# A top-k search over experts moved from 80 lists on partitions to 125 nodes on partitions, with its ranks and its list products rearranged

## What is computed

```python
x = x + gnn(layernorm(x), src, dst, edge_attr, ...)   # 41250 edges, messages summed per node
h = layernorm(x)
S = softmax(h @ Wg, axis=-1)                          # 1250 nodes x 8 experts
G, I = top_k(S.T, 312)                                # for each expert its 312 highest nodes
ex = h[I]                                             # 8 x 312 x 512
out = gelu(ex @ W1[e] + b1[e]) @ W2[e] + b2[e]        # 512 -> 1024 -> 512
x = x.at[I].add(G[..., None] * out)
```

## Time and profile before

| what | value |
|---|---|
| median of 3 runs | 1441.53 us (1441.02 to 1441.79) |
| the profiled execution | 1442.35 us |
| its span in the trace | 1440.5 us |
| TensorE matmul busy | 1323.8 us, 92% |
| VectorE busy | 1027.4 us, 71% |
| mean granted TensorE clock | 0.951 |
| search, first to last instruction | 1078.10 to 1108.64 us |
| ranks, to the end of `pos` | to 1116.03 us |
| first product of the first expert | 1132.35 us |

### The profile page before, as it was taken

The page is one execution under the profiler, slowest core; times in us unless marked ns, Lnnn a source line. Parts: engine busy times, 40 slices in busy tenths (PEclk is TensorE's granted clock), DMA queues, the critical chain, the costliest instruction groups (busy, mean ns, idle before and its releaser), DMA issues. The chain is left out here.

```text
span 1440.5 us, 26692 instructions
## 1 busy us (share of the span) xinstructions
PE 1323.8 (92%) x7075; PEld 791.9 (55%) x7075; DVE 1027.4 (71%) x2512; ACT 816.6 (57%) x2049; POOL 799.3 (55%) x843
## 2 busy tenths in 40 slices
PE   5786799999999999999999999999962799999997
PEld 1463456656555556555555555555561455555553
DVE  7869589999999899999999999998776311111110
ACT  3769667777777777777777777777550111111111
POOL 5258577777777777777777777777200122222211
PEclk7689899999999999999999999999995799999998
DMA  7315033444443444444443333434452155555421
GB/s 246 162 44 162 20 113 113 123 130 123 126 127 110 129 124 127 127 132 136 123 115 109 110 114 109 115 109 112 65 189 71 58 164 163 163 163 162 145 37 18
DMA packets 65870, 172.45 MB, mean 120 GB/s; under 512 B 14260, under 2 KB 22820, under 8 KB 65191
## 3 DMA queue, kind: packets, MB, share of 16 engines
q0 software_dynamic: 43424, 105.53, 27.9%
q1 hardware_dynamic: 22398, 66.38, 13.4%
HBM read 148.53 MB, written 18.08 MB: 116 GB/s over the span
## 5 line engine op out<-in xcount | busy, mean ns | idle before, releaser
L1130 PE MATMUL PS<-prod,oneh 128*64 128x256 f32 x2052 | 469.6, 382 | 4.0 <-DVE region_s L944 2.0
L564 POOL DMA_INDIRECT recs<-rec_d,inv_i x342 | 323.2, 945 | 113.0 <-issue 81.0
L575 POOL DMA_INDIRECT gath<-table_d,recs x342 | 323.5, 946 | 106.0 <-issue 78.7
L1130 PEld LDWEIGHTS PS<-prod,oneh 128*64 128x64 f32 x2052 | 268.9, 137 | 199.4 <-issue 77.7
L707 ACT ACTIVATE oneh<-oneh,recs 128x64 f32<-128x64 f32 x1026 | 282.2, 338 | 145.7 <-DVE oneh L921 143.8
L1123 PE MATMUL PS<-prod,oneh 128*64 128x256 f32 x1368 | 356.1, 392 | 0.0
L1111 PE MATMUL PS<-wf_sb,h_t 128*128 128x512 f32 x684 | 333.2, 610 | 2.9 <-DVE h_t L907 2.9
L932 DVE TENSOR_TENSOR prod<-PS,gath 128x768 f32<-128x768 f32 x342 | 324.9, 950 | 0.0
L944 DVE TENSOR_TENSOR region_s<-region_s,PS 128x512 f32 x342 | 232.6, 680 | 17.9 <-issue 13.6
L714 ACT COPY PS<-c_rep 128x512 f32<-128x512 f32 x338 | 190.4, 583 | 79.0 <-DVE prod L932 78.6
L930 DVE TENSOR_TENSOR prod<-PS,gath 128x256 f32<-128x256 f32 x342 | 143.9, 421 | 54.6 <-DMA gath<-table_d,recs 38.7
(11 more groups left out here) (264 smaller groups left out, 1503.8 us busy)
## 6 DMA issues: line engine op xcount, KB each, us to landing
region_r<-wu SPq DMA_DIRECT2D x16, 512.0 KB, 4.3
region_r<-wd SPq DMA_DIRECT2D x16, 512.0 KB, 5.6
region_u<-wu SPq DMA_DIRECT2D x16, 512.0 KB, 4.3
region_u<-wd SPq DMA_DIRECT2D x16, 512.0 KB, 5.8
recs<-rec_d,inv_i POOLq DMA_INDIRECT x342, 2.6
gath<-table_d,recs POOLq DMA_INDIRECT x342, 3.3
region_u<-rec_in SPq DMA_DIRECT2D x1, 5168.0 KB, 16.1
rec_d<-region_u SPq DMA_DIRECT2D x1, 5168.0 KB
```

Source lines behind the costliest of these rows:

```text
L564: nc.gpsimd.indirect_dma_start(out=recs[:, q % RING, k, :], out_offset=None, in_=rec_d, in_offset=bass.IndirectOffsetOnAxis(ap=inv_i[:, t: ...
L575: nc.gpsimd.indirect_dma_start(out=gath[:, t % GRING, :], out_offset=None, in_=table_d, in_offset=bass.IndirectOffsetOnAxis(ap=recs[:, q % ...
L1130: return nc.tensor.matmul(to, oneh[:, slot, 1 + i, :], prod[:, slot, P_Q:P_B + i + 1:1 + i, :], start=i == 0, stop=i == 2, skip_group_chec ...
```

## The change

- `SEARCH` goes from 15 to 10 steps and each step fixes three bits: eight candidates, seven compared (`LEVELS` = 8). The candidates now stand on every node partition, [125, 8, 8]; one VectorE instruction compares all of `probs` with all seven ([125, 7, 10, 8], 560 elements a partition, bf16 output `over`). The count is ten TensorE products, one for each place t, of an all-ones 125 x 125 bf16 matrix `ones_h` with `over[:, :, t, :]` (56 columns), accumulated; they give the sums on all 125 partitions. `probs_t`, `same`, `same_lo`, `rsel` and the transposition go.
- The constants of the search, `ones_h` and `ident_h` are set at the start of the second block's VectorE code, where `rsel` was, and `pos` is filled with 4096.
- The ranks: two compares of [125, 80] into `took` (above, equal), one sum over t (`tied`), and one round of TensorE: nine products with the identity for the running sum over t (`took[:, :, t]` repeated for all later places, 144 down to 16 columns), one with `lower_h` for the nodes of lower partitions, one with `ones_h`. Two predicated copies write `pos`.
- `list_of` takes place t outside and chunk c inside, and waits for each one-hot apart: `l_oh` is raised by every one-hot, not by the tenth.

```diff
-SEARCH, UNROLL = 15, 5
+SEARCH, UNROLL = 10, 5
+LEVELS = 8
...
+        over = node_h[:, 0:(LEVELS - 1) * GE // 2].bitcast(BF16).rearrange("p (k t e) -> p k t e", k=LEVELS - 1, t=BLOCKS)
+        took = node_h[:, at_took:at_took + GE].bitcast(BF16).rearrange("p (m t e) -> p m t e", m=2, t=BLOCKS)
+        ones_h, ident_h = (prod_f[0:BP, k * WIDE:(k + 1) * WIDE].bitcast(BF16)[:, 0:BP] for k in range(2))
...
+                link(nc.vector.tensor_copy(ones_h, ones[0:BP, 0:BP]))
+                link(nc.vector.tensor_copy(ident_h, ident[0:BP, 0:BP]))
+                adds = cand[:, 1, :, :]
+                link(nc.vector.memset(thr[:, :], 0))
+                for k in range(LEVELS):
+                    link(nc.vector.memset(cand[:, 1, k, :], k << (3 * SEARCH - 3)))
+                link(nc.vector.memset(pos[:, :, :], 4096.0))
                 dve.wait_ge(s_x1, 16 * BLOCKS)
-                dve.wait_ge(s_bu, 16)
-                link(nc.vector.tensor_copy(rsel[:, :].rearrange("k (t e) -> k t e", e=EXPERTS),
...
-                link(nc.vector.tensor_copy(same[:, :], PS[0:GE, 3, 0:GE]))
-                link(nc.vector.tensor_tensor(same_lo[:, :], same[:, :], lower[0:GE, 0:GE], ALU.mult))
                 link(nc.vector.tensor_copy(bu_col[:, :], PS[:, 2, 0:EXPERTS * FK]))
...
-                dve.wait_ge(g_ps, 2)
-                link(nc.vector.tensor_copy(probs_t[:, :], PS[0:GE, 3, 0:BP]))
...
                 def search_step(i):
...
-                    for k in range(1, 4):
-                        last = nc.vector.tensor_scalar(sel[:, k, :], probs_t[:, :], cand[:, 0, k:k + 1].bitcast(F32), None,
-                                                       ALU.is_ge, ALU.add, accum_out=bcnt[:, k - 1:k])
-                    last.then_inc(b_cnt, 1)
-                    nc.vector.tensor_scalar(adds, adds, 2, None, ALU.logical_shift_right)
+                    nc.vector.tensor_tensor(over, probs[:, :, :].unsqueeze(1).to_broadcast([BP, LEVELS - 1, BLOCKS, EXPERTS]),
+                                            at_each_node(levels.bitcast(F32), [BP, LEVELS - 1, BLOCKS, EXPERTS]),
+                                            ALU.is_ge).then_inc(b_cnt, 1)
+                    nc.vector.tensor_scalar(adds, adds, 3, None, ALU.logical_shift_right)
...
+                limit = thr[:, :].bitcast(F32).unsqueeze(1).to_broadcast([BP, BLOCKS, EXPERTS])
+                nc.vector.tensor_tensor(took[:, 0], probs[:, :, :], limit, ALU.is_gt)
+                link(nc.vector.tensor_tensor(took[:, 1], probs[:, :, :], limit, ALU.is_equal))
                 dve.sem_inc(g_pr, 1)
...
+                    link(nc.vector.tensor_reduce(tied[:, :, :], took.rearrange("p m t e -> p m e t"), AX.X, ALU.add))
                 dve.sem_inc(g_pr, 1)
...
+                for m in (1, 0):
+                    link(nc.vector.copy_predicated(by_node, took[:, m].bitcast(mybir.dt.int16),
+                                                   PS[0:BP, 3, m * GE:(m + 1) * GE].rearrange("p (t e) -> p t e", e=EXPERTS)))
...
-                        nc.tensor.matmul(PS[0:GE, 6, 0:3], same[:, :], bcnt[:, 0:3], start=True, stop=True
-                                         ).then_inc(b_sum, 1)
+                        for t in range(BLOCKS):
+                            last = nc.tensor.matmul(PS[0:BP, 6, 0:(LEVELS - 1) * EXPERTS].rearrange(
+                                "p (k e) -> p k e", e=EXPERTS), ones_h, over[:, :, t, :], start=t == 0, stop=t == BLOCKS - 1)
+                        last.then_inc(b_sum, 1)
...
+                for t in range(BLOCKS - 1):
+                    nc.tensor.matmul(ranks[:, :, t + 1:, :], ident_h,
+                                     took[:, :, t:t + 1, :].to_broadcast([BP, 2, BLOCKS - 1 - t, EXPERTS]),
+                                     start=t == 0, stop=False, skip_group_check=True)
...
-                        last = nc.vector.tensor_scalar(rank_oh[:, t, :], iota_h[0:BP, :], rank, None, ALU.is_equal)
-                    last.then_inc(l_oh, 1)
+                        nc.vector.tensor_scalar(rank_oh[:, t, :], iota_h[0:BP, :], rank, None, ALU.is_equal).then_inc(l_oh, 1)
...
-                    pe.wait_ge(l_oh, e + 1)
-                    for c in range(RCH):
-                        for t in range(BLOCKS):
+                    for t in range(BLOCKS):
+                        pe.wait_ge(l_oh, BLOCKS * e + t + 1)
+                        for c in range(RCH):
```

More of the change, by code:

```diff
@@ L395, in build @@
         red = sb("red", [BP, 2, BLOCKS])
[L396 to L403, removed]
+        thr = sb("thr", [BP, EXPERTS], I32)
+        cand = sb("cand", [BP, 2, LEVELS, EXPERTS], I32)
+        tied = sb("tied", [BP, 2, EXPERTS], BF16)
+        node_h = h_t[0:BP, :, :].rearrange("p a b -> p (a b)")
+        over = node_h[:, 0:(LEVELS - 1) * GE // 2].bitcast(BF16).rearrange("p (k t e) -> p k t e", k=LEVELS - 1, t=BLOCKS)
+        at_took = (LEVELS - 1) * GE // 2
+        took = node_h[:, at_took:at_took + GE].bitcast(BF16).rearrange("p (m t e) -> p m t e", m=2, t=BLOCKS)
+        ones_h, ident_h = (prod_f[0:BP, k * WIDE:(k + 1) * WIDE].bitcast(BF16)[:, 0:BP] for k in range(2))
         pos = sb("pos", [BP, EXPERTS, BLOCKS])
@@ L1310, in _, with at_each_node @@
                 dve.sem_inc(g_pr, 1)
-                dve.wait_ge(g_ps, 2)
-                link(nc.vector.tensor_copy(probs_t[:, :], PS[0:GE, 3, 0:BP]))
[L1314 to L1317, removed]
+                def at_each_node(levels, shape):
+                    return levels.unsqueeze(2).to_broadcast(shape)
                 def search_step(i):
-                    nc.vector.tensor_tensor(cand[:, 0, :], thr[:, :].to_broadcast([GE, 4]), adds,
-                                            ALU.bitwise_or).then_inc(b_ch, 1)
+                    levels = cand[:, 0, 1:, :]
+                    nc.vector.tensor_tensor(cand[:, 0, :, :], thr[:, :].unsqueeze(1).to_broadcast([BP, LEVELS, EXPERTS]),
+                                            adds, ALU.bitwise_or).then_inc(b_ch, 1)
@@ L1340, in _ @@
                         search_step(UNROLL * i + n)
-                above, equal, before, take, rank, s5 = (sel[:, k, :] for k in range(6))
-                thr_f = thr[:, :].bitcast(F32)
-                link(nc.vector.tensor_scalar(above, probs_t[:, :], thr_f, None, ALU.is_gt, ALU.add,
-                                             accum_out=bcnt[:, 0:1]))
-                link(nc.vector.tensor_scalar(equal, probs_t[:, :], thr_f, None, ALU.is_equal))
-                link(nc.vector.tensor_tensor_scan(s5, equal, equal, 0.0, ALU.add, ALU.bypass))
@@ L1364, in _ @@
-                link(nc.vector.tensor_copy(pos[:, :, :], PS[0:BP, 3, 0:GE].rearrange("p (t e) -> p e t", e=EXPERTS)))
+                limit = thr[:, :].bitcast(F32).unsqueeze(1).to_broadcast([BP, BLOCKS, EXPERTS])
+                nc.vector.tensor_tensor(took[:, 0], probs[:, :, :], limit, ALU.is_gt)
+                link(nc.vector.tensor_tensor(took[:, 1], probs[:, :, :], limit, ALU.is_equal))
+                dve.sem_inc(g_pr, 1)
+                with nc.allow_low_precision(reason="counts up to ten"):
+                    link(nc.vector.tensor_reduce(tied[:, :, :], took.rearrange("p m t e -> p m e t"), AX.X, ALU.add))
```

54 lines of the change are left out of this document (18 added, 36 removed).

## The result

| kernel | median of its runs | lowest to highest | ratio to before, 95% interval |
|---|---|---|---|
| before | 1441.32 us (5 runs) | 1440.82 to 1441.79 | |
| after | 1434.15 us (5 runs) | 1433.09 to 1435.92 | 0.9958 (0.9946 to 0.9970) |

The change saves 7.2 us by the medians, 6 us by the ratio. The forecast was 1432.5 us, a gain of 9. The profiled execution took 1434.7 us, its span is 1432.9.

The account below looks back on a forecast made before the run. Search, ranks and list 0, where TensorE is not the bound, move the end one for one. Terms -2.0 - 1.9 - 4.5 - 0.7 = -9.1 us gave 1432.5 us; range 1425 to 1438.

Parts of the forecast that it names:

- Head: Between softmax and search: transposition, copy, memsets, same and same_lo go, constants move to idle time at block start; -2.0 us.
- Pace of the ten products: Search step's TensorE count: products bound by loading 125 bf16 columns at clock 0.50, 0.105 us apart, 1.28 us until VectorE's use.
- The rival of fast products: Search and tail: weight load hides behind streaming, pace 0.047 us, search 22.6 us, total 1425.8 us; chance 0.17 including a raised clock.
- f32-like loads: Search and tail: the products pay what f32 weights pay, 0.21 us each; 1444.0 us, no change; chance 0.08.
- the slower rival without overlap: Search products pay load plus streaming, 0.21 + 0.047 us each; search 43.3 us, total 1449 us; chance 0.06.
- Compare: Search step on VectorE: comparing 560 elements at the plain per-element slope takes 0.73 us.
- Search: Ten steps of 2.81 us and one loop return at 0.5: 28.6 us against 30.5, so -1.9 us.
- Tail: From the search's end to pos written: 2.9 us for 7.39, predicated copies at 0.27 us each; -4.5 us.
- List 0: First list: VectorE's wait for the thirty products falls from 1.06 to 0.3 us; -0.7 us.
- Lists in the loop: Six lists in the expert loop: added waits and register instructions hidden by the sequencer's lead; 0, bound 0 to +3 us.
- Clock: First expert's start at clock 0.50, costing 1.95 us, is left as it is by the change; 0.
- The lost-gain rival: VectorE or loops: compare at twice the price (+7) or register instructions exposed (+3); 1435.5 to 1439.5 us; chance 0.13.

Follow-up runs that it names:

- e4: Changed kernel with ones_h, ident_h and lower_h loaded with 128 columns instead of 125; 1429.83 us, ratio 0.9929 to before.
- e7: Changed kernel with 128 columns, one wait per list in the expert loop, search without loop, pos as [place, expert]; 1628.36 us, before on that chip 1641.18.
- e2: The changed kernel run once more, unaltered, with a second profile; 1433.90 us, ratio 0.9962 to before.
- e9: Kernel before with only the list part of the change (a wait per one-hot, place outside); 1443.33 us, ratio 1.0011 to before.
- e3: Changed kernel, but the six lists in the expert loop wait once for all ten one-hots; 1431.56 us, ratio 0.9939 to before.
- e5: Changed kernel, but lists in the expert loop have one register wait and nine waits for constants reached long ago; 1634.18 us, before on that chip 1641.18.
- the two controls: The kernel before and the changed kernel, each run again unaltered with a second profile; 1440.14 and 1433.90 us.
- e8: e7 plus TensorE products nobody reads, before and during the search, around the first lists and during the gathers; 1621.18 us, before on that chip 1641.18.
- e10: e8 with 21 instead of 16 unread products during the gathers and more among the first transpositions; 1422.03 us, before on that chip 1442.49.

## Why the prediction was right, and where its terms were off

- **Head, -2.0:** -1.94 (6.16 to 4.22). The constants were hidden, as priced: from the second block's start to the softmax 35.56 and 35.60.
- **Pace of the ten products, 0.105 us:** right. They start 0.107 us apart; with the way to VectorE they take 1.31 us for the 1.28 forecast. e4 shows that the load sets them. The value was a middle between two ends, 0.047 and 0.21, and half of the f32 row; that the bytes set the load is not what e4 shows, where 128 columns of the same type load in about half the time of 125. The rival of fast products is what 128 columns give: 0.65 us, a search of 23.86 where the rival had 22.6. f32-like loads and the slower rival without overlap are excluded by the same row.
- **Compare, 0.73:** 0.742 us (median of ten); the four-level broadcast operands cost nothing beyond the plain slope.
- **Search, -1.9:** only -0.6. No single term failed. The decision and the maximum take 0.22 and 0.27, together 0.55 with their gaps where 0.49 stood; the products and the compare give 0.05 more. 2.91 for 2.81 in ten steps is 1.0 us. The loop's return takes 0.5 as forecast, and the first two steps are 0.14 and 0.20 us longer than the rest.
- **Tail, -4.5:** -4.2. Products and sum as forecast (1102.68 to 1104.15 is 1.47 us, forecast 1.45). The mis-sized term is the predicated copy, 0.27 forecast, 0.494 measured. The copy writes with a stride of ten elements; where e7 writes consecutive ones it takes 0.247.
- **List 0, -0.7:** -0.73, wait 0.34 for the 0.3 forecast.
- **Lists in the loop, 0 with bound 0 to +3:** the step that failed. "The sequencer is ahead", it said, and "4.2 us of lead against 0.5 to 1 us of new work: I price it at 0". The lists cost +3.4 us (e2, e4, e9 and after: period 38.08 to 38.23 for 37.54): 2.5 for the waits on register values, shown by e3 and e5, and 0.9 with the order of places. The lead was real for the list's head: in the kernel after, its first register instructions run at 1138.3 us, its products at 1142.5. But it is a lead in places, not in time. The sequencer got four places ahead and then stood until the list began, and the other five places cost it 0.22 us each beside products of 0.075, as the rows under e5 show. That 9 x 55 ns = 0.5 us came near the measured 0.42 is chance: such an instruction takes 0.09 us to the next, and only those count that the sequencer had not done ahead.
- **Clock, 0:** no run shows the change moving it, but it was not nothing in the number. The first block and the first expert moved by -4.2 and +1.1 in these two profiles, and by -1.5 and -0.4 in the two controls.
- **Sum:** the change's own stages give -1.9 - 0.6 - 4.2 - 0.7 + 3.4 = -4.0, half of the -9.1. Timed, the ratios of after and e2 give -6.1 and -5.5 us, with intervals from -7.8 to -4.3 and from -7.8 to -3.3. The forecast of 1432.5 lay 1.65 us from the median although three terms missed 5 us between them (search 1.3, tail 0.3, lists 3.4). The timed gain is 1.5 to 3.2 us above the stages'. In the profiles such a surplus lies in the first block, whose code is the same; for the timed runs no trace shows where it lies. That the total fits better than the terms is luck.
- **The lost-gain rival** was half right: register instructions exposed, at 2.5 us for the +3 it named, though the compare was not dearer.

## What to carry to other kernels

Before you count small products, look at the number of columns of the stationary operand: padding 125 to 128 halved ten bf16 products at clock 0.50 and gave 6.5 us in the search and the tail, more than the change itself by its own stages. Don't put a wait with a register value between short products because the sequencer "is ahead": compare what a place costs the sequencer with what its products take, and look how many places it gets ahead. Wait once at the head, or for constants. Where a chain of small steps leaves TensorE nearly idle ahead of dense work, products that nobody reads can pay: 3.2 us in e8, where they kept the search at full clock, and 4.3 in e10, where they reached up to the first expert but also stood in its way.

## What was unexpected of the hardware

- A reached wait for a constant between products adds nothing measurable (0.84 us for 30 products with nine of them); nine whose values are in registers add 0.42 us at full clock. It is no price of each wait: the first seven places keep their pace and the last three are late.
- A predicated copy of 80 f32 elements: 247 ns to consecutive elements, 494 ns with a stride of ten.
- 32 products of layer two take 13.84 us behind a list with the chunk outside, 13.95 to 13.97 with the place outside, and 13.93 with no list ahead. Open.
- The same first block ended between 1031.13 us (e4, granted clock 1.00 from 70 to 110 us) and 1036.38 (before, 0.87). What moves the clock there is open. Nor was the fall in e10 expected: it came at 1098 us after 1095 to 1097 with 0.13 and 0.46 us of TensorE work, whereas e8 kept 1.00 through a microsecond with none (1297 to 1298).
